# Attention products of a gated cross-attention kernel in two 16-bit halves instead of two rounded 32-bit halves

## The reference, cut to what matters

```python
def _L0_xattn_ref(x, latents, key_padding_mask, kv_gate, ..., Wq, Wk, Wv, Wout):
    x = layernorm(x, gamma_media, beta_media)          # context, 375 rows
    latents = layernorm(latents, gamma_lat, beta_lat)  # 112 rows
    kv = jnp.concatenate((x, latents * kv_gate), axis=1)
    q = (latents @ Wq).reshape(b, n, HEADS, DIM_HEAD)
    k = (kv @ Wk).reshape(b, f + n, HEADS, DIM_HEAD)
    v = (kv @ Wv).reshape(b, f + n, HEADS, DIM_HEAD)
    sim = jnp.einsum('bqhd,bkhd->bhqk', q * SCALE, k)
    ...                                                # masked
    attn = jax.nn.softmax(sim, axis=-1)
    out = jnp.einsum('bhqk,bkhd->bqhd', attn, v).reshape(b, n, HEADS * DIM_HEAD)
    return out @ Wout

x = x + jnp.tanh(g_xattn[0]) * _L0_xattn_ref(ctx_1024, _layernorm(x), mask, ...)
x = x + jnp.tanh(g_ffn[0]) * _L0_ffn_ref(_layernorm(x), ...)   # 8 experts, top 2
```

## Time and profile before

| | |
|---|---|
| median of 3 executions | 1739.65 us (1735.29 to 1740.99) |
| profiled execution, its own time | 1738.3 us |
| its span, first to last instruction | 1736.7 us |
| mean granted TensorE clock | 0.955 |
| PE matmul / weight load busy | 1558.6 us / 1329.2 us |
| DVE / ACT / POOL busy | 948.8 / 838.3 / 613.7 us |

### The profile page before, as it was taken

One profiled execution on the slowest core, in us unless ns is written; L12 is line 12 of the kernel. 1 busy time (PEld: TensorE's weight loads), 2 busy tenths in 40 slices (PEclk: granted clock), 3 DMA queues, 4 the chain that ended last, 5 costly groups with the idle time before them and its releaser, 6 DMA issues.

```text
span 1736.7 us, 39641 instructions
## 1 busy us (share of the span) xinstructions
PE 1558.6 (90%) x11946; PEld 1329.2 (77%) x11947; DVE 948.8 (55%) x2655; ACT 838.3 (48%) x1856; POOL 613.7 (35%) x663
## 2 busy tenths in 40 slices
...
PEclk9899999899999999999999976999999999999987
...
GB/s 92 46 105 112 93 114 106 137 98 83 144 85 96 129 108 115 89 146 89 85 142 75 101 145 237 261 76 27 27 27 27 170 259 82 30 26 29 27 235 84
DMA packets 70908, 180.59 MB, mean 104 GB/s; under 512 B 11664, under 2 KB 33552, under 8 KB 70864
## 3 DMA queue, kind: packets, MB, share of 16 engines
...
## 4 chain that ended last, share of the span: by engine, by line
PE 68%; DMA 9%; DVE 8%; issue 7%; ACT 3%; another core or an unknown queue 2%; POOL 2%; SPq 1%; DVEq 0%; POOLq 0%; ACTq 0%
PE fP L1185 21%; PE yP L1185 9%; PE gP L1185 9%; PE uP L1185 8%; DMA W<-split_experts 5%; PE simP L1233 4%; PE ptP L1243 4%; PE oP L1185 3%; PE aP L1371 3%; PE tP L1185 2%; DMA out<-ysb,xt 2%; PE fP L1201 1%; DMA xt<-routed_rows 1%; DMA mraw<-mask 1%
## 5 line engine op out<-in xcount | busy, mean ns | idle before, releaser
L1185 PE MATMUL fP<-zTs,ws 128*128 128x112 f32 (+1 forms) x1536 | 308.2, 353 | 27.7 <-DVE zT L811 27.3
L1185 PEld LDWEIGHTS fP<-zTs,ws 128*128 128x128 f32 x1536 | 242.5, 202 | 74.7 <-ACT zT L611 29.2
L1124 DVE TENSOR_TENSOR act_h<-uP,sg 128x512 f32<-128x512 f32 x126 | 87.2, 692 | 291.3 <-ACT sg L732 291.3
L1185 PE MATMUL gP<-W,xT 128*128 (+1 forms) x756 | 210.0, 414 | 35.4 <-issue 27.7
L732 ACT ACTIVATE sg<-gP 128x512 f32<-128x512 f32 x126 | 75.3, 598 | 292.2 <-PE uP L1185 292.2
L1185 PE MATMUL fP<-ws,zTs 128*122 128x512 f32 x768 | 207.6, 406 | 4.7 <-DVE kT L824 4.7
L1185 PEld LDWEIGHTS yP<-W,aT 128*128 128x128 f32 x1512 | 192.1, 194 | 10.1 <-issue 5.3
L1185 PE MATMUL yP<-W,aT 128*128 (+1 forms) x1512 | 194.0, 285 | 4.6 <-DVE aT L1128 4.6
L548 POOL DMA_INDIRECT out<-ysb,xt x63 | 100.6, 1596 | 275.5 <-ACT ysb L744 260.5
L1185 PE MATMUL uP<-W,xT 128*128 (+1 forms) x756 | 197.3, 397 | 0.0
L636 ACT ACTIVATE pr<-ms,nmax 112x488 f32<-112x488 f32 x256 | 179.7, 702 | 18.5 <-DVE nmax L834 18.5
...
## 6 DMA issues: line engine op xcount, KB each, us to landing
...
```

The costliest lines, as they stand in the source:

```text
L1124: nc.vector.tensor_tensor(act_h[i][:, :], uP[i][:, :], sg[i][:, :], ALU.mult).then_inc(s_act, 1)
L1185: last = nc.tensor.matmul(o, lhs(k, a), rhs(k, c), start=n == 0, stop=n == len(todo) - 1)
```

## The change

All operands of the attention's products become two fp16 halves: `kT`, `qT`, `zTs`, `ws`, `aoT`. So that they fit fp16's range, each weight and the layernorm's gains are scaled by powers of two, from bounds that the prologue computes (sums of squares on ACT, summed over partitions by one matmul with ones, then an inverse square root on POOL, cut to a power of two on DVE). ACT's high copies of q, k and v take a constant scale 1/`TOP`, and DVE's low halves become one scalar-tensor-tensor instruction in place of a tensor-tensor one. The scores are scaled back in `masked_max`, by a value per partition in SBUF (`sim_undo`) where a constant stood. `qT` and the stationary of a v piece are widened to 128 columns. The weights' high halves go from DVE to ACT.

```diff
-V_TOP = 2.0 ** 13
+TOP = 2.0 ** 14
...
-        kT[0] = sb("kT0", [P, 2, MB, NK], F32R, pa)
+        kT[0] = sb("kT0", [P, 2, MB, NK], F16, pa)
-        qT[0] = sb("qT0", [P, 2, MB, S], F32R, pa)
-        zTs = [sb(f"zTs{i}", [P, 2, KD, TC], F32R, pa) for i in range(2)]
+        qT[0] = sb("qT0", [P, 2, MB, P], F16, pa)
+        zTs = [sb(f"zTs{i}", [P, 2, KD, TC], F16, pa) for i in range(2)]
...
-        ws = sb("ws", [P, 2, 4, KD * INNER], F32R, pa)
+        ws = sb("ws", [P, 2, 4, KD * INNER], F16, pa)
...
-        aoT = sb("aoT", [P, 2, MB, S], F32R, pa)
+        aoT = sb("aoT", [P, 2, MB, S], F16, pa)
...
             # GpSimd
+            rstd(0)
+
+            pool.wait_ge(s_sch, 3)
+            nc.gpsimd.tensor_tensor(small[:, :], bound[:, :], minus_half[:, 0:5], ALU.pow).then_inc(s_small, 1)
             mask_bias(0, 0)
-            rstd(0)
             rows_lo(0, 0)
...
             # ScalarE
-            nc.scalar.activation(absln[:, 0:2, :], lnv[:, 0:2, :], ACT.Abs)
-            nc.scalar.activation(absln[:, 2:4, :], lnkv[:, :, :], ACT.Abs)
+            nc.scalar.activation(lnsq[:, 0:2, :], lnv[:, 0:4:2, :], ACT.Square, scale=LN_MAX, accum_out=sq[:, 4:5])
...
             act.wait_ge(s_wld, 64)
-            nc.scalar.activation(absw, wr[:, 2, :], ACT.Abs).then_inc(s_abs, 1)
+            for i in range(4):
+                last = nc.scalar.activation(wsq[:, i, :], wr[:, i, :], ACT.Square, accum_out=sq[:, i:i + 1])
+            last.then_inc(s_squares, 1)
+            def weights_hi(i):
+                act.wait_ge(s_fit, 1)
+                nc.scalar.activation(ws[:, 0, i, :], wr[:, i, :], ACT.Copy, scale=fit[:, i:i + 1]).then_inc(s_wsplit, 1)
...
-                nc.scalar.activation(o, i, ACT.Copy).then_inc(s_phi, 1)
+                nc.scalar.activation(o, i, ACT.Copy, scale=1.0 / TOP).then_inc(s_phi, 1)
...
             for part in range(2):
                 norm_rows(0, 0, part)
+            for i in range(2):
+                weights_hi(i)
             rows_out(0)
             rows_hi(0, 0)
+            for i in range(2, 4):
+                weights_hi(i)
...
             # VectorE
-                nc.vector.tensor_tensor(o, i, hi, ALU.subtract).then_inc(s_plo, 1)
+                nc.vector.scalar_tensor_tensor(out=o, in0=i, scalar=1.0 / TOP, in1=hi, op0=ALU.mult, op1=ALU.subtract).then_inc(s_plo, 1)
...
-                nc.vector.tensor_tensor_reduce(out=ms[h % 2][:, :], in0=simP[h % 2][0:S, 0:NK], in1=madd[p][:, :], scale=-SCALE,
+                nc.vector.tensor_tensor_reduce(out=ms[h % 2][:, :], in0=simP[h % 2][0:S, 0:NK], in1=madd[p][:, :], scale=sim_undo[0:S, 0:1],
...
-            for i in (0, 1, 3):
-                last = nc.vector.tensor_copy(ws[:, 0, i, :], wr[:, i, :])
...
+            def weights_lo(i):
+                dve.wait_ge(s_wsplit, i + 1)
+                return nc.vector.scalar_tensor_tensor(out=ws[:, 1, i, :], in0=wr[:, i, :], scalar=fit[:, i:i + 1], in1=ws[:, 0, i, :],
+                                                      op0=ALU.mult, op1=ALU.subtract)
+
+            dve.wait_ge(s_bound, 1)
+            slink(1, nc.vector.tensor_reduce(bound[:, 4:5], simP[0][:, 4:8], AX.X, ALU.add))
...
+            weights_lo(0)
+            weights_lo(1).then_inc(s_wready, 1)
+            dve.wait_ge(s_fit, 3)
             latents_out(0)
+            weights_lo(2)
+            weights_lo(3).then_inc(s_wready, 1)
             norm_stats(1, 1)
...
             # TensorE
-                    last = product(o[0:KR, 0:INNER], lambda k, a: zTs[p][:, a, k, c * KR:(c + 1) * KR],
+                    last = product(o[:, 0:INNER], lambda k, a: zTs[p][:, a, k, c * KR:c * KR + P],
...
-                        last = nc.tensor.matmul(simP[i][0:S, 0:NK], qT[p][r, a, h // 2, :], kT[p][r, c, h // 2, :],
+                        last = nc.tensor.matmul(simP[i][:, 0:NK], qT[p][r, a, h // 2, :], kT[p][r, c, h // 2, :],
...
-            for k in range(KD):
-                last = nc.tensor.matmul(simP[0][:, 0:INNER], ones[:, :], absw[:, k * INNER:(k + 1) * INNER], start=k == 0, stop=k == KD - 1)
-            last.then_inc(s_vsum, 1)
+            pe.wait_ge(s_squares, 1)
+            nc.tensor.matmul(simP[0][:, 0:8], ones[:, :], sq[:, :], start=True, stop=True).then_inc(s_bound, 1)
```

More of the change, by code:

```diff
@@ L157, in build @@
         ones = sb("ones", [P, P], F32, pa)
-        absln = sb("absln", [P, 4, KD], F32, pa)
-        reach = sb("reach", [P, 2, KD], F32, pa)
-        vmax = sb("vmax", [P, 1], F32, pa)
-        vscale = sb("vscale", [P, 1], F32, pa)
+        lnsq = sb("lnsq", [P, 6, KD], F32, pa)
+        sq = sb("sq", [P, 8], F32, pa)
+        bound = sb("bound", [P, 5], F32, pa)
+        small = sb("small", [P, 5], F32, pa)
+        fit = sb("fit", [P, 5], F32, pa)
+        held = sb("held", [P, 3], F32, pa)
+        twice = sb("twice", [P, 2], F32, pa)
+        undo = sb("undo", [P, 2], F32, pa)
+        sim_undo = sb("sim_undo", [P, 1], F32, pa)
         earlier = sb("earlier", [S, S], F32, pa)
@@ L608, in rows_out @@
                 need(act, s_zsplit, b)
+                if isinstance(b, int) and b == 0:
+                    act.wait_ge(s_fit, 2)
                 for k in range(KD):
@@ L646, in heads_out_hi @@
                 act.wait_ge(s_aot, b + 1)
-                nc.scalar.activation(aoT[:, 0, :, :], aoT_P, ACT.Copy).then_inc(s_aohi, 1)
+                nc.scalar.activation(aoT[:, 0, :, :], aoT_P, ACT.Copy, scale=1.0 / P_TOP).then_inc(s_aohi, 1)
             def norm2_out(b):
@@ L856, in heads_out_lo @@
                 dve.wait_ge(s_aohi, b + 1)
-                nc.vector.tensor_tensor(aoT[:, 1, :, :], aoT_P, aoT[:, 0, :, :].bitcast(F32), ALU.subtract).then_inc(s_aolo, 1)
+                nc.vector.scalar_tensor_tensor(out=aoT[:, 1, :, :], in0=aoT_P, scalar=1.0 / P_TOP, in1=aoT[:, 0, :, :],
+                                               op0=ALU.mult, op1=ALU.subtract).then_inc(s_aolo, 1)
             def residual(b, p):
@@ new lines, in slink @@
+            def slink(n, ins):
+                ins.then_inc(s_sch, 1)
+                dve.wait_ge(s_sch, n)
+            def weights_lo(i):
[4 more added lines that the diff above has]
+            slink(1, nc.vector.tensor_reduce(bound[:, 4:5], simP[0][:, 4:8], AX.X, ALU.add))
```

78 lines of the change are left out of this document (32 added, 46 removed).

## The result

| | before | changed |
|---|---|---|
| median | 1739.35 us (1735.29 to 1740.99, 4 runs) | 1635.16 us (1632.20 to 1638.28, 4 runs) |
| ratio of the times, 95% interval | | 0.9407 (0.9388 to 0.9427) |
| profiled execution, its own time | 1738.3 us | 1634.2 us |
| its span | 1736.7 us | 1632.5 us |
| mean granted clock | 0.955 | 0.971 |

Forecast were 1706 us, 1670 to 1732. The kernel is faster, as forecast, but by 104 us where I had 32.5.

A forecast was written before the change was run, and what follows sets the result against it. PE was taken to bound only part of a pair; DVE and a scatter-tied pause bound the rest. 13 pairs at -1.85 us (-24), first pairs -8.5, last batches -3, prologue +3: -32.5 us, so 1706 us, range 1670 to 1732.

The forecast's parts named there:

- Bounds and pace: Attention matmuls on PE: near one column per cycle in fp16, saving 3.6 us of PE time a batch.
- Rival D: Attention matmuls: only short ones get cheaper, those of 488 and 512 columns keep their pace; 1726 us, chance 0.20.
- (a): From k0 after the pause to DVE's stretch in the odd batch: PE sets the pace; -2.6 us, between 1.56 and 3.8.
- (b): Odd batch, from DVE's stretch to `slot_i`: DVE's work stays, only its wait of 1.72 us shrinks; -0.25 us a pair.
- (d): `masked_max` reads its factor per partition, 70 ns more each, about half on the path: +0.55 us a pair.
- Prologue: Start of the kernel: extra ACT squares and copies and DVE low halves delay batch 1; +3 us, from -1 to +6.
- The two pairs without a pause: Batches 0 to 3: no pause, so each pair gains 4.2 us, together -8.5 us.
- (c): From `slot_i` to k0 after the pause: cheaper q and scores only make PE wait longer; gain 0, bounds 0 and 2 us.
- (e): At k0 and k1 after the pause: longer idleness keeps the clock at 1.2 GHz longer; +0.45 us a pair.
- Rival E: Even batch, idle stretch ahead of k0: it lengthens, clock stays at 1.2 GHz far beyond k1; slower, 1745 us, chance 0.10.
- B: Pause ahead of k0: not tied to the scatter but begins or ends with PE's progress; 1680 us, chance 0.15.
- C: Whole attention: TensorE is the bound throughout, 3.6 us saved in each of 30 batches; about 1633 us, chance 0.05.

The follow-up runs named there:

- a_const: The changed kernel with a constant as the scale of `masked_max`, scaling back of the scores left out: 1631.95 us, ratio 0.9375 to the kernel before.
- a_narrow: The changed kernel without the two widenings to 128 columns (122 for v pieces, 112 for scores): 1641.59 us, ratio 0.9431 to the kernel before.
- a_q3_even_2: The changed kernel with the q pieces of even batches made three times over, on a pausing chip: 1702.27 us, ratio 0.9782 to the kernel before.

## Why the prediction was wrong

*Bounds and pace: right.* Long fp16 matmuls run at the column rate (207 and 215 ns forecast 205 and 215), q at 50 ns. Rival D is out. Only the scores were too hopeful, 0.72 us for 0.62.

*(a), PE's stretch, -2.6:* the interval that answers to it is 3.12 us shorter, inside the bounds of (a). It isn't (a) alone: `masked_max` is in it, and so is the clock at k0 and k1, which before had low (below). The pause costs the changed kernel 0.7 us there (25.29 us on a pausing chip, 24.59 on a calm one), and before about as much by difference (52 / 13 - 3.2 = 0.8). *(b), -0.25:* the interval is 0.29 us shorter. *(d), +0.55:* `a_const` shows 0.39 us a pair. *Copies, 0:* right (615 ns both times). *Prologue, +3:* 3.85. *The two pairs without a pause, -4.2 each* (their own terms, -1.85 - 2 - 0.45, give -4.3): measured -4.3 each. *The last batches, -3:* of the 6.8 us between the loop's end and the expert stage 5.4 are the thirteenth pair, so some 1.4 us. On the calm chip all pairs are without a pause, and there 15 x -4.2, less 3, plus 3 would have been -63 us against -56.7 measured.

*The step that failed is (c)*, "from `slot_i` to the k0 after the pause nothing is gained", with the bounds of 0 and 2 us: it measured -4.16 us a pair; and the pair got 7.6 us shorter, where the prediction had named 4 us as the sign that it was wrong. I had read the end of the pause as tied to the scatter, which fits every trace that has a pause, and concluded that zT is released at a fixed time behind `slot_i` whatever PE does. But a pause has a beginning too, and a signal that PE gives ahead of it arrives at once (ACT starts zT 0.04 us behind the first transposes, at 613.85 us). Before, the two pairs of transposes of `rows_T` ended 3.6 and 4.1 us behind `slot_i` and fell in. With q pieces of 1.19 us in place of 2.73 they end 2.7 and 3.1 us behind it (the first 613.81 - 611.14) and are through in all 12 pairs. The edge isn't sharp: `a_narrow` has the second one at the same 3.1 us and takes it late in 6 of 12 pairs, and the q piece of `a_q3_even_2` is late at 2.7 us. The scatter's data begin to move at 2.7 us. The 2 us that were to make PE wait longer carry it past the edge: -0.96 us of work (5.28 to 4.32) and -3.2 us of pause. I had bounded a threshold effect by the size of the work that moved.

*(e) fell with it.* I had +0.45 us for a longer time at 1.2 GHz behind a longer idle stretch. There is no idle stretch ahead of k0 now, the clock in the window of 613.85 to 618.55 us is 1.00, and the 4.24 us of k0 and k1 became 2.64 us for the same 12 matmuls. Start to start they take 2.48 us (618.10 - 615.62), 207 ns each. Rival E is out for the same reason.

*B and C.* B doubted the right sentence, but its mechanism (a pause that follows PE) is contradicted by the table above, and its 1680 us were 45 too many. That C's number, 1633 us, is nearly what came out is luck; its mechanism isn't what happened: TensorE's work gives 4.3 us a pair and not 7.2 (before's 61.95 less the 52/13 = 4.0 us that it loses to the pause, less 53.67), and the rest is the pause. On the calm chip C would have said 105 us less than 1688, 1583 us, where 1631 were measured.
